# The list of the first expert tiles is made a block sooner, and the routing of the last three blocks moves between the expert tiles

## The reference

```python
router_logits = xf @ router_w.T
probs = softmax(router_logits)
topv, topi = top_k(probs, 2)
probs = probs * mask_of(topi)
probs = probs / (probs.sum(-1) + 1e-9)
g = einsum('nd,edf->nef', xf, gate_w) + gate_b
u = einsum('nd,edf->nef', xf, up_w) + up_b
y = einsum('ne,ned->nd', probs, einsum('nef,efd->ned', silu(g) * u, down_w) + down_b)
```

## Time and profile before

| what | value |
|---|---|
| median of three runs | 1710.3 us (1709.44 to 1716.64) |
| profiled execution | 1718.21 us, its span 1716.4 us |
| TensorE (PE) busy | 1523.2 us, 89% of the span |
| VectorE (DVE) busy | 1087.5 us, 63% |
| ScalarE (ACT) busy | 724.6 us, 42% |
| GpSimd (POOL) busy | 677.0 us, 39% |
| mean granted clock of TensorE | 0.942 of full |

### The profile page before, as it was taken

One profiled execution on the slowest core, in us unless ns is written; L12 is line 12 of the kernel. 1 busy time (PEld: TensorE's weight loads), 2 busy tenths in 40 slices (PEclk: granted clock), 3 DMA queues, 4 the chain that ended last, 5 costly groups with the idle time before them and its releaser, 6 DMA issues. The chain is left out here.

```text
span 1716.4 us, 30448 instructions
## 1 busy us (share of the span) xinstructions
PE 1523.2 (89%) x10698; PEld 1079.5 (63%) x10698; DVE 1087.5 (63%) x2352; ACT 724.6 (42%) x1572; POOL 677.0 (39%) x530
## 2 busy tenths in 40 slices
PE   6999954899999999957999999997798999999980
PEld 3555523788888887633677777776555666666650
DVE  4899866577777874531557777888555444454443
ACT  4877751234434444543455455552242222222224
POOL 1354447222333311010344566654545544444440
PEclk9999975699999999988999999998899999999995
DMA  3233446645555535053034124110733322323326
GB/s 105 87 144 114 160 149 185 181 107 163 151 161 137 155 72 186 35 200 120 15 99 138 31 74 145 50 37 13 255 56 38 47 47 44 50 44 46 49 35 202
DMA packets 186939, 177.15 MB, mean 103 GB/s; under 512 B 79639, under 2 KB 147787, under 8 KB 186667
## 3 DMA queue, kind: packets, MB, share of 16 engines
q1 hardware_dynamic: 163963, 145.23, 28.1%
q0 software_dynamic: 17216, 22.95, 8.1%
q10 hardware_dynamic: 5616, 7.08, 1.2%
HBM read 111.19 MB, written 64.01 MB: 102 GB/s over the span
## 5 line engine op out<-in xcount | busy, mean ns | idle before, releaser
L2476 POOL DMA_INDIRECT y<-vw,idx x71 | 125.5, 1768 | 190.7 <-DVE vw L2622 180.3
L622 DVE SCALAR_TENSOR_TENSOR conv_y<-conv_in,taps,conv_y 128x512 f32<-128x512 f32 x192 | 161.4, 850 | 24.2 <-ACT conv_y L470 19.5
L1867 PE MATMUL xQ<-late,last 128*128 128x512 f32 x256 | 128.5, 625 | 8.9 <-ACT late L2029 4.8
L2540 PE MATMUL xO<-late,aT 128*128 x568 | 135.4, 381 | 0.8 <-DVE vw L2620 0.8
L2519 PE MATMUL xS<-w_gu,kT 128*128 x288 | 132.2, 602 | 0.8 <-ACT kT L2566 0.6
L375 PE MATMUL ps_j<-xnT,w_qkv 128*128 128x512 f32 x256 | 122.4, 602 | 0.0
L1815 POOL TENSOR_TENSOR sc<-sc,den 128x1232 f32<-128x1232 f32 x32 | 72.0, 2250 | 113.6 <-DVE den L2286 113.5
L2607 DVE TENSOR_TENSOR sc<-xS,last 128x512 f32<-128x512 f32 x107 | 73.7, 692 | 60.6 <-PE xS L2519 57.2
L2540 PEld LDWEIGHTS xO<-late,aT 128*128 128x128 f32 x568 | 103.1, 192 | 12.5 <-issue 1.2
L2620 DVE TENSOR_TENSOR vw<-xO,late 128x256 f32<-128x256 f32 x71 | 30.1, 424 | 121.4 <-PE xO L2540 121.4
L996 POOL DMA_DIRECT2D x<-x1t x32 | 18.2, 568 | 223.5 <-ACT x1t L1348 218.4
(11 more groups left out here) (354 smaller groups left out, 3675.1 us busy)
## 6 DMA issues: line engine op xcount, KB each, us to landing
carried<-qkvg SPq DMA_DIRECT2D x64, 256.0 KB, 4.0
qkvg<-tok SPq DMA_DIRECT2D x4, 2048.0 KB, 6.7
qkvg<-gate SPq DMA_DIRECT2D x8, 1024.0 KB, 9.5
qks<-qkvg SPq DMA_DIRECT2D x32, 256.0 KB, 4.6
steps<-step SPq DMA_DIRECT2D x30, 256.0 KB, 4.4
qkvg<-carried SPq DMA_DIRECT2D x3, 2048.0 KB, 6.5
vw<-even SPq DMA_DIRECT2D x4, 1232.0 KB
xin<-in_x SPq DMA_DIRECT2D x9, 512.0 KB, 10.0
```

The source lines that it names most:

```text
L622: y = nc.vector.scalar_tensor_tensor(conv_y[m % 4][:], conv_in[b][:, m, k:k + BT], taps[:, m, k:k + 1], conv_y[m % 4][:], ALU.mult, ALU.add)
L1867: mm = pe.matmul(Q[:], w_q[:, c, j * P:(j + 1) * P], x1T[:, c, :], start=c == 0, stop=c == KD - 1)
L2476: nc.gpsimd.indirect_dma_start(out=s["y"].rearrange("t p d -> (t p) d"), out_offset=bass.IndirectOffsetOnAxis(ap=x.idx[j % 8][:, 0:1], axi ...
L2540: mm = pe.matmul(x.pD[:, 0:D], x.hT[q][:, k, :], w_d[:, bass.ds(e, 1), k, :], start=k == 0, stop=k == FK - 1)
```

## The change

`HEAD_BLOCKS` becomes 4, so that `HEAD` becomes 24 and the rest 47 tiles; `head_list` runs in block 5. `entries(5)`, `top_two(6)` and `counts(6)` leave block 7 and its end and go between the expert tiles 0 to 2, `listed_rows(5)` goes there in two groups of four transfers, and the steps of the last two blocks come later than before.

```diff
--- before.py
+++ after.py
@@ -37,7 +37,7 @@
 FK = FF // P
 ENT = 4
 FT = (TILES * P * 2) // P + NE - 1
-HEAD_BLOCKS = BLOCKS - 3
+HEAD_BLOCKS = BLOCKS - 4
 HEAD = (HEAD_BLOCKS * BLK * P * 2 - NE * (P - 1)) // P
 REGION = TILES + 1
 SPARE = (NE * (P - 1) + NE * REGION + P - 1) // P
@@ -1831,16 +1831,18 @@
                         add_mask(g + 1)
                     if n and t == 0:
                         x2_deviations(n - 1)
-                    if n >= 2 and t in (1, 2):
+                    if 2 <= n < BLOCKS - 1 and t in (1, 2):
                         listed_rows(n - 2, (2 * t - 2, 2 * t - 1))
 
             def between(j):
                 if j == 0:
                     x2_deviations(BLOCKS - 1)
-                if 2 <= j < 2 + BLK:
-                    listed_rows(BLOCKS - 2, (j - 2,))
-                if 9 <= j < 9 + BLK:
-                    listed_rows(BLOCKS - 1, (j - 9,))
+                if j in (1, 2):
+                    listed_rows(BLOCKS - 3, (2 * j - 2, 2 * j - 1))
+                if 4 <= j < 4 + BLK:
+                    listed_rows(BLOCKS - 2, (j - 4,))
+                if 10 <= j < 10 + BLK:
+                    listed_rows(BLOCKS - 1, (j - 10,))
 
             expert_gpsimd(nc, pool, x, s, between)
             pool.wait_ge(list_out, 16 * BLOCKS * BLK * 2)
@@ -2003,15 +2005,16 @@
                         queries(m, jobs[2])
                     if t == 2 and n == BLOCKS - 1:
                         logits(n - 1, X).then_inc(lg_done, 1)
-            pe.wait_ge(lg_sb, BLOCKS - 1)
-            counts(BLOCKS - 2, X).then_inc(cn_done, 1)
 
             def between(j):
-                if j in (1, 2):
-                    x2_turned(BLOCKS - 1, j - 1)
-                if j == 3:
+                if j == 2:
+                    pe.wait_ge(lg_sb, BLOCKS - 1)
+                    counts(BLOCKS - 2, X).then_inc(cn_done, 1)
+                if j in (3, 4):
+                    x2_turned(BLOCKS - 1, j - 3)
+                if j == 5:
                     logits(BLOCKS - 1, X).then_inc(lg_done, 1)
-                if j == 6:
+                if j == 8:
                     pe.wait_ge(lg_sb, BLOCKS)
                     counts(BLOCKS - 1, X).then_inc(cn_done, 1)
 
@@ -2120,9 +2123,9 @@
             def between(j):
                 if j == 0:
                     x2_norm(BLOCKS - 1)
-                if j in (1, 2):
-                    x2_out_of_psum(BLOCKS - 1, j - 1)
-                if j == 4:
+                if j in (3, 4):
+                    x2_out_of_psum(BLOCKS - 1, j - 3)
+                if j == 6:
                     weights_exp(BLOCKS - 1)
 
             expert_scalar(nc, act, x, s, between)
@@ -2345,9 +2348,9 @@
                         logits_out(n - 1, X)
                     if t == 2 and n:
                         shifted_logits(n - 1)
-                    if t == 3 and n:
+                    if t == 3 and 0 < n < BLOCKS - 1:
                         top_two(n - 1)
-                    if t == 0 and n >= 2:
+                    if t == 0 and 2 <= n < BLOCKS - 1:
                         entries(n - 2)
                     if t and n == HEAD_BLOCKS + 1:
                         head_list(t - 1)
@@ -2355,21 +2358,25 @@
             def between(j):
                 if j == 0:
                     norm_terms(BLOCKS - 1)
+                    entries(BLOCKS - 3)
+                if j == 1:
+                    top_two(BLOCKS - 2)
+                if j == 2:
                     dve.wait_ge(cn_done, 1)
                     counts_out(BLOCKS - 2, X)
-                if j == 1:
+                if j == 3:
                     entries(BLOCKS - 2)
-                if j == 4:
+                if j == 6:
                     dve.wait_ge(lg_done, 2)
                     logits_out(BLOCKS - 1, X)
                     shifted_logits(BLOCKS - 1)
-                if j == 5:
+                if j == 7:
                     top_two(BLOCKS - 1)
-                if j == 7:
+                if j == 9:
                     dve.wait_ge(cn_done, 2)
                     counts_out(BLOCKS - 1, X)
                     entries(BLOCKS - 1)
-                if j == 8:
+                if j == 10:
                     rest_list()
 
             def last_residual():
```

## The result

The changed kernel takes 1717.7 us (median of 18 runs, 1712.9 to 1722.8), the kernel before on the same chips 1713.1 us (18 runs). The ratio is 1.0029, with a 95% interval of 1.0017 to 1.0042: 2.9 to 7.2 us slower, where 5.4 us were forecast. That is clear of noise, and under the 0.5% that was called no change.

What follows compares the result with a forecast made beforehand. TensorE bounds block 5 and the expert tiles, the softmax chain block 6. Terms -0.6 + 3.7 + 0.4 - 0.5 + 2.4 = +5.4 us on 1710.3 gave 1715.7 us; range over all cases 1704 to 1722.

Steps and rivals of the forecast that it cites:

- Step 1: Head list moved from block 6 to 5: +4.5 us in block 5, -5.1 in block 6, net -0.6 us.
- Rival C: Block 5's lag is not given back in block 6: 1720.8 us, slower by 0.61%; chance 0.15.
- Step 2: entries(5) and eight list writes leave block 7: chain 2.8 us shorter, attention ends some 3.4 us earlier with Step 1.
- one of the signs that I had named: TensorE's idle before the first expert transpose would be 6 us instead of 3.2.
- Step 3: top_two(6) leaves block 7's end: rows behind the weights hold the experts' start, which moves only by -0.6 us.
- rival A: Row loads not held behind the weights, experts start some 6.6 us earlier: 1707 us; chance 0.13.
- Step 4: Routing between the expert tiles: gather 5 late behind list writes, TensorE waits +3.7 us at tile 5.
- rival B: The eight list writes hide and gather 5 lands in time, no wait or clock loss: 1709.6 us; chance 0.19.
- the walk: Estimated times of VectorE, GpSimd and TensorE through the first expert tiles, with gather 5 at 1268.2 in old-trace time.
- The term for the clock: After the wait at tile 5, TensorE's first eight expert matmuls run at half clock: +2.4 us.
- The -0.5 us for an old wait: TensorE's 0.48 us wait for the x2 rows would go, since these transposes stand two tiles later.
- The later stall behind the rest list: TensorE's 2.56 us stall for a gather late behind list writes comes again in the same order: no cost.

Runs made afterwards that it cites:

- e3: The changed kernel with the head list made in block 6 again, the moved routing staying; ratio 1.0035 to the kernel before.
- e4: The kernel before with only the head list moved to block 5; ratio 0.9996 to the kernel before.
- e5: The kernel before with top_two(6) moved behind expert tile 0, and counts(6) with it; ratio 1.0087 to the kernel before.
- e11: The kernel before with only GpSimd's order changed, list writes before the scatter; ratio 0.9967 to the kernel before.
- e7: e1 with the first eight expert tiles' row loads issued in front of the late weights; ratio 1.0012 to the kernel before.
- e1: The changed kernel with entries(5) and its eight list writes back in block 7; ratio 0.9974 to the kernel before.
- e10: e1 with GpSimd's list writes before the scatter; ratio 0.9965 to the kernel before.
- e2: The changed kernel with block 5's list writes spread two by two after expert tiles 1 to 4, later steps moved to match; ratio 1.0038 to the kernel before.
- e8: The changed kernel with only entries(5) back in block 7, its list writes staying among the expert tiles; ratio 1.0026 to the kernel before.
- e9: The changed kernel with GpSimd's list writes before the scatter instead of behind it; ratio 0.9967 to the kernel before.
- e12: e9 with the first six tiles' rows loaded first, then gate and up biases, then down weights; ratio 0.9937 to the kernel before.

## Why the prediction was right

- **Step 1, the head list**: forecast +4.5 us in block 5 and -5.1 in block 6; the chain shows +4.2 and -5.1, and the ScalarE wait that was to swallow 0.6 us did. The missing 0.3 is the narrower list, which I had given nothing: its four wide instructions take 2.62, 0.35, 0.36 and 0.35 us for the 2.69, 0.42, 0.42 and 0.42 of before. e3 and e4 confirm that the move nets to almost nothing (0.1 and -0.5 us). Rival C falls with them and with the 0.36 us of wait for GpSimd that is left in block 6.
- **Step 2, block 7's chain**: shorter as forecast. Its last sum stands at 1210.98, 111.7 us from the mark, against 115.6 before. The last attention matmuls start 4.1 us earlier but end only 1.3 us earlier, and not some 3.4: they took 7.34 us at a granted clock of 0.62, where the kernel before took 4.59. So TensorE's idle in front of the experts did not grow to 6 us, one of the signs that I had named: it is 3.01 against 3.17. The slower matmuls cost nothing, since the rows were later still.
- **Step 3, the start**: the rows behind the weights hold it, as read from the landing of 14.1 us. e5 and the 8.91 us wait of the casts show it, and rival A falls: its 6.6 us did not come. The size was off: the first transpose came 1.8 us earlier, not 0.6. Some 0.9 of it is the weights' earlier issue (94.8 against 95.7 us from the mark), the rest a load that took 0.9 us less: 29.8 us from the first weights' issue to the landing of the first rows, against 30.7. The first eight matmuls also took 5.39 us and not the 6.10 of before, another 0.7 that the sum does not have.
- **Step 4, the writes**: the wait at tile 5 was forecast at 3.7 us and is 4.07, so rival B falls too. The gather of tile 5 starts 159.7 us from the mark, and the walk, with its -0.6, had 159.6. It was a little pessimistic on the gather's length: started at 1258.96, it is used at 1262.26, 3.3 us later, where I took 4.1. TensorE came there sooner. The term for the clock, +2.4, measured 2.7: from 1262.26 to 1267.74 it is 5.48 us, where the same instructions at full clock take 2.8 (0.2 for the transposes, 0.4, 1.7 and 0.4 for the groups behind, by their distances before the wait).
- **Terms left out or wrong**: counts(6) waited 0.69 us for the pick, which the sum does not have, and it was 0.87 us from its start to the next matmuls, where I took 0.4. The -0.5 us for an old wait did not come: the gate matmuls of tile 2 waited 0.83 us for ScalarE, where 0.48 + 0.25 stood before, so this term is +0.1. The later stall behind the rest list came again as said: waits of 0.59, 1.44, 2.50 and 0.64 us, 5.2 us together, against 0.48, 0.44, 1.30, 2.56 and 0.46 before, also 5.2.
- The sum of 5.4 us stands against 5.8 at the last group and 5.0 timed. Its mechanism is borne out: no gain at the start from top_two, a wait at tile 5, and the clock behind it. That the number is so close is in part luck: the start was better by 1.2 and 0.7 us, and against it stand 1.2 us of counts(6), 0.6 of the old wait, 0.4 of the new one and 0.3 of the clock, 0.6 us more in all.
- What I did not see is that the wait hung on the order of two calls on GpSimd, and that the old kernel paid for the same order: the stalls that I carried over as given cost it 4.8 us (e11).

The Trainium skill, "DMA: Bandwidth & Descriptors", section "Queues, rings and completion order", says that a transfer's semaphore increment is a strongly ordered write, which lands only after every earlier write of that DMA engine, across its queues. The traces agree with it: the same 2 KB load lands 14.1 and 14.6 us after its issue behind the weights, and in 2.2 us (median of eight) ahead of them in e7. No run here tells this rule from a queue whose data simply drain in order.

## What to carry to other kernels

In a queue that works in order, put the work that depends on nothing before the instruction that waits, not behind it: the swap was worth 10.9 us to the changed kernel and 4.8 to the one before, and the eight moved writes, which cost 6.4 us in one place, cost nothing that shows in the other. Before moving a step out of a critical end, look whether something else, such as a small load behind a large one, lands at the same moment; if it does, mend that first, and then look at what lands next (rows first alone gave nothing in the timed runs, rows and biases first gave 5.8 us at the last group). Where executions differ by more than the effect, compare profiles from a mark just ahead of the change.

## What the runs showed of the hardware

- Small transfers get in the way of a large load. In the six profiles with the list writes of block 5 in block 7 (before, e1, e4, e5, e10, e11) the first transpose is at 129.8 to 131.2 us from the mark, mean 130.6; in the five without them that load in the same order (changed, e2, e3, e8, e9) at 128.5 to 129.8, mean 129.1. The eight writes, 2 KB each, seem to cost the 9 MB load 1.4 us. It is the load and not its start that differs: its first issue stands at 94.8 to 95.9 us in both groups. The pair that parts it best is e1 and e8, which differ only in where these writes are: 130.3 and 129.4, one execution each, so the 1.4 us is an estimate from the means.
- SyncE takes 1.1 us for each small load that reads its address from the list (8.9 us for eight in e7, 6.7 for six in e12), so that issuing them early moves everything behind them: the first down weights are issued 105.5 us from the mark in e7 and 94.9 in e1.
